# Retention block and FP4 feed-forward: block division on GpSimd, exponents later on VectorE, x rounded in the even body, 11 weight pieces

## What is computed

```python
def fp4_quant_dequant(x):                      # blocks of 16 along the last dim
    xb = x.reshape(shape[:-1] + (shape[-1] // 16, 16))
    scale = jnp.maximum(jnp.max(jnp.abs(xb), -1, keepdims=True) / 6.0, 1e-12)
    xn = xb / scale
    idx = jnp.searchsorted(_MID, jnp.abs(xn))  # nearest of 0 .5 1 1.5 2 3 4 6
    return (_GRID[idx] * jnp.sign(xn) * scale).reshape(shape)

x = layernorm(x + retention(x))                # (2, 2048, 256), 8 heads of 32 / 64
h = silu(q(x) @ q(w_gate).T) * (q(x) @ q(w_up).T)      # q = fp4_quant_dequant
x = layernorm(x + q(h) @ q(w_down).T)          # hidden width 704
```

## Time and profile before

| | |
|---|---|
| median of three runs | 673.51 us |
| the profiled execution | 673.45 us, span 671.5 us |
| busy, share of the span | TensorE matmul 588.0 us (88%), VectorE 580.9 (87%), ScalarE 335.6 (50%), GpSimd 187.3 (28%) |
| attention loop, window 240 to 280 us | TensorE busy 39.79 of 40, VectorE 37.26, ScalarE 26.70, GpSimd 15.29, granted TensorE clock 1.00 |
| feed-forward loop, window 520 to 560 us | TensorE 36.03 of 40, VectorE 38.47, clock 1.00 |

### The profile page before, as it was taken

One profiled execution on the slowest core, in us unless ns is written; L12 is line 12 of the kernel. 1 busy time (PEld: TensorE's weight loads), 2 busy tenths in 40 slices (PEclk: granted clock), 3 DMA queues, 4 the chain that ended last, 5 costly groups with the idle time before them and its releaser, 6 DMA issues.

```text
span 671.5 us, 14647 instructions
## 1 busy us (share of the span) xinstructions
PE 588.0 (88%) x4290; PEld 502.6 (75%) x4290; DVE 580.9 (87%) x1439; ACT 335.6 (50%) x869; POOL 187.3 (28%) x230
## 2 busy tenths in 40 slices
PE   3179999999999999999999677779988999999965
PEld 2158888788787878788787566669877888888755
DVE  6056889999999999999998779989999999999996
ACT  3125656666575666666575643224434334433332
POOL 1011124334533444334530203232222222222110
PEclk9779999999999999999999798979999999999998
DMA  6471101110111001110110000000000000000001
GB/s 155 55 230 41 32 25 49 47 39 8 47 47 47 23 23 47 47 39 8 47 31 18 8 8 2 1 0 19 28 16 16 16 16 16 16 16 16 17 16 48
DMA packets 25853, 23.11 MB, mean 34 GB/s; under 512 B 2024, under 2 KB 22760, under 8 KB 25832
## 3 DMA queue, kind: packets, MB, share of 16 engines
q1 hardware_dynamic: 25016, 21.27, 11.3%
q10 hardware_dynamic: 816, 1.57, 0.7%
HBM read 17.56 MB, written 5.28 MB: 34 GB/s over the span
## 4 chain that ended last, share of the span: by engine, by line
DVE 23%; PE 18%; issue 9%; ACT 1%; POOL 1%; DVEq 1%; ACTq 0%; POOLq 0%
PE wide_banks L1182 9%; PE upd_y L1182 5%; DVE shared L800 2%; DVE stats L926 2%; DVE shared L922 2%; DVE shared L993 1%; PE wide_banks L1340 1%; DVE h_amax L782 1%; DVE shared L989 1%; DVE win_lo L913 1%; DVE shared L795 1%; DVE win_lo L910 1%; DVE h_inv L791 1%; DVE h_scale L787 1%; POOL shared L1160 1%
## 5 line engine op out<-in xcount | busy, mean ns | idle before, releaser
L1160 POOL TENSOR_TENSOR shared<-shared,h_scale 128x704 f32<-128x704 bf16 x32 | 44.4, 1387 | 202.5 <-DVE shared L805 196.9
L1182 PE MATMUL wide_banks<-wgu_hi,xq_hi 128*128 128x512 f32 (+1 forms) x192 | 65.1, 421 | 27.8 <-DVE xq_lo L982 27.8
L1182 PE MATMUL wide_banks<-win_hi,x_hi 128*128 128x512 f32 x192 | 68.5, 438 | 12.9 <-DVE win_lo L885 11.0
L442 ACT ACTIVATE shared<-opened,rstd 128x64 f32<-128x64 f32 x256 | 64.7, 335 | 11.0 <-DVE rstd L715 10.7
L413 ACT ACTIVATE shared<-shared 128x704 bf16<-128x704 f32 x32 | 25.3, 790 | 83.4 <-DVE shared L795 83.4
L1241 PEld LDWEIGHTS mixed<-shared 128*128 128x128 f32 x512 | 62.0, 192 | 2.8
L1182 PE MATMUL wide_banks<-win_hi,x_lo 128*128 128x512 f32 x192 | 60.8, 398 | 0.0
L1182 PE MATMUL wide_banks<-win_lo,x_hi 128*128 128x512 f32 x192 | 60.8, 398 | 0.0
L1241 PE MATMUL mixed<-shared 128*128 128x64 f32 x512 | 60.6, 271 | 0.0
L1182 PEld LDWEIGHTS wide_banks<-wgu_hi,xq_hi 128*128 128x128 f32 x192 | 33.1, 200 | 36.0 <-DVE xq_lo L982 33.0
L1182 PE MATMUL wide_banks<-wgu_hi,xq_lo 128*128 128x512 f32 (+1 forms) x192 | 58.9, 389 | 0.0
(11 more groups left out here) (146 smaller groups left out, 1496.3 us busy)
## 6 DMA issues: line engine op xcount, KB each, us to landing
xf<-in_x_feat SPq DMA_DIRECT2D x32, 128.0 KB, 2.2
tab<-in_tables SPq DMA_DIRECT2D x16, 256.0 KB, 2.7
xt<-in_x_tok SPq DMA_DIRECT2D x32, 128.0 KB, 2.1
out<-shared SPq DMA_DIRECT2D x32, 128.0 KB, 1.7
x<-in_w_in ACTq DMA_DIRECT2D x3, 512.0 KB, 5.3
w<-in_w_gu SPq DMA_DIRECT2D x1, 1408.0 KB, 7.8
pow_dram<-powers SPq DMA_DIRECT2D x1, 1056.0 KB
w<-in_w_down SPq DMA_DIRECT2D x1, 704.0 KB, 9.1
```

Source lines behind the costliest of these rows:

```text
L442: last = act.activation(gated[:, b, cols], opened[:, b, cols], ACT.Copy, scale=rstd[:, b, 1 + k:2 + k])
L1160: pool.tensor_tensor(over_blocks(hq[:, b]), over_blocks(h_steps[:, b]), spread(h_fp4["scale"][:, b]), ALU.mult).then_inc(h_fp4["ready"], 1)
L1182: last = pe.matmul(dst, lhs, rhs, start=k == 0, stop=k == len(parts) - 1)
```

## The change

Nothing of what is computed changes. `x_unit` and `w_unit` go from VectorE to GpSimd, in odd bodies behind `split_x`. On VectorE `w_exponent` comes behind the rotation, `x_exponent` behind `apply_gate`. On ScalarE `round_w_from` comes behind `square_heads`; `round_x_from`, with `round_x1` on GpSimd, goes from the odd body to the even body after it, still between `normalise_heads` and `copy_v`. The loop begins at tile 8, so there are 11 pieces of 384 columns. Behind the loops the steps for the last tiles are moved accordingly.

```diff
-LOOP_FROM, LOOP_TO = 3, TILES // 2 - 1
+LOOP_FROM, LOOP_TO = 4, TILES // 2 - 1
...
 # ScalarE, body
-                if piece is not None and b == 1:
-                    round_w_from(piece)
                 if in_turn(n - LAG):
                     copy_gatedT(n - LAG)
...
                 if valid(n - 2):
                     normalise_heads(n - 2, b)
-                if b == 1 and tiles_of(n - 1):
-                    round_x_from(n - 1)
+                if b == 0 and tiles_of(n - 2):
+                    round_x_from(n - 2)
                 if valid(n + 1):
                     copy_v(n + 1, 1 - b)
...
                 if valid(n):
                     square_heads(n)
+                if piece is not None and b == 1:
+                    round_w_from(piece)
...
 # VectorE, body
-                if w and b == 1:
-                    w_unit(piece)
-                    w_exponent(piece)
                 if valid(n):
                     decay_scores(n)
...
-                if x:
-                    x_unit(n - 1)
-                    x_exponent(n - 1)
                 if valid(n + 1):
                     rotate_products(n + 1, 1 - b)
                     rotate_sum(n + 1, 1 - b)
                 if w and b == 0:
                     w_max(piece)
+                if w and b == 1:
+                    w_exponent(piece)
                 if valid(n):
                     apply_gate(n, b)
...
+                if x:
+                    x_exponent(n - 1)
                 if in_turn(n - LAG):
                     add_resid(n - LAG, 1 - b)
...
 # GpSimd
+            def x_unit(n):
+                need(pool, x_fp4["ready"], n - 4)
+                pool.wait_ge(x_fp4["step"], FP4_STEPS // 2 * (n - 4) + 3)
+                pool.tensor_tensor(over_blocks(x_fp4["unit"][:, 0, 0:width(n)]), over_blocks(columns(x1_flat, n)),
+                                   spread(x_fp4["inv"][:, 0:width(n) // BLOCK]), ALU.mult).then_inc(x_fp4["step"], 1)
+
+            def w_unit(piece):
+                pool.wait_ge(w_fp4["step"], FP4_STEPS * piece + 3)
+                pool.tensor_tensor(over_blocks(w_fp4["unit"][:, 0]), over_blocks(w4[:, bass.ds(piece * PIECE, PIECE)]),
+                                   spread(w_fp4["inv"][:]), ALU.mult).then_inc(w_fp4["step"], 1)
...
 # GpSimd, body, behind decay_k and split_x
                 if piece is not None and b == 1:
+                    w_unit(piece)
+                if b == 1 and tiles_of(n - 1):
+                    x_unit(n - 1)
+                if piece is not None and b == 1:
                     round_w4(piece)
-                if b == 1 and tiles_of(n - 1):
-                    round_x1(n - 1)
+                if b == 0 and tiles_of(n - 2):
+                    round_x1(n - 2)
```

## The result

The changed kernel takes 682.4 us (median of four runs, 680.25 to 683.87), the kernel before on the same chip 673.66 (673.32 to 674.2): ratio 1.0126, 95% interval 1.0095 to 1.0157. It is slower, by 8.7 us where 15.3 were forecast.

A forecast was written before the change was run, and what follows sets the result against it. TensorE's 10.55 us pace and VectorE's hand-overs were taken as the bound. Bodies of 11.15 and 11.85 make pairs +1.41, eleven times +15.5, less 0.2: +15.3 on 673.45, so 688.7 us; range 673 to 692.5.

The forecast's parts named there:

- the forecast case: Whole kernel: the outcome the prediction held likeliest, 685.5 to 692 us, chance 0.52.
- The two hand-overs: VectorE to TensorE: decay_scores to project_v is free up to 3.10 us, decay_q to turn_gated up to 2.12.
- the 0.51 between L617 and L1265 was chance: Doubt that TensorE really waits for decay_q before turn_gated; it decides the rival of freed VectorE time, chance 0.09.
- VectorE's time was the bound and is freed: Rival for the loop: both bodies run at 10.55 us, −5.9 us in all, 667.6 us; chance 0.09.
- The late squares: Even body: x's rounding ahead of square_heads adds 0.54, apply_gate starts 0.98 before the odd body, q becomes 2.88.
- The stall at `split_x` in the odd body: VectorE's L736 waits for GpSimd's split_x: +0.54, q 3.42, odd body 11.85 us.
- x_exponent behind L1134: End of body: x_exponent, issued 0.12 too late, waits for GpSimd's first add; L632 starts at −0.35 instead of −1.09.
- GpSimd's queue in the even body: Add, scale, decay_k and split_x delay VectorE's joint chain: decay_scores at 3.7 instead of 2.99, even body 11.15 us.
- only the stall at `split_x` is missing: Rival: even body 11.15, odd 11.31, so pair +0.87 and 682.9 us, range 680 to 685.5; chance 0.16.
- Tile 7's body: Tiles 6 and 7 have no weights with 11 pieces of 384: about −0.2 us.
- outside the pairs: Edges: tile 31's last rounding of x moves into the start of the feed-forward part; taken as 0, ±1 us.
- the clock is no term: TensorE: its work per pair stays, busy some 21 of 23 us, so no clock cost was counted.

The follow-up runs named there:

- e1: Changed kernel with x's rounding on ScalarE moved ahead of normalise_heads in the even body; 683.73 us, ratio 1.0143.
- e2: Changed kernel with x_exponent ahead of apply_gate instead of behind it; 679.64 us, ratio 1.008.
- e3: Changed kernel with x's rounding ahead of normalise_heads, x_exponent ahead of apply_gate, and decay_q ahead of the two reciprocals; 675.16 us, ratio 1.0012.
- e4: Changed kernel with w_scale and w_inverse moved from the odd body to the even one, right behind w_max; 697.82 us, ratio 1.0349.
- e6: Changed kernel with one GpSimd line added: split_x of tile n+2 waits for decay_scores of tile n; 673.29 us, ratio 0.9983.
- e8: Changed kernel with split_x held until decay_scores and x_exponent ahead of apply_gate; 671.87 us, ratio 0.9969.
- e9: Changed kernel with split_x held until decay_scores, x_exponent ahead of apply_gate and decay_q ahead of the two reciprocals; 668.3 us, ratio 0.9917.
- e7: Changed kernel with x's rounding ahead of normalise_heads, x_exponent ahead of apply_gate, decay_q ahead of the reciprocals, and split_x held until decay_scores; 666.43 us, ratio 0.9881.
- e5: Kernel before with one GpSimd line added: split_x of tile n+2 waits for decay_scores of tile n; 670.61 us, ratio 0.9949.
- b1: Kernel before with 11 weight pieces of 384 columns and x's rounding (ScalarE and GpSimd) moved to the even body; 682.74 us, ratio 1.0126.

## Why the prediction was right, and where its sizes were off

The mechanism came as forecast, its size didn't. The measured 682.4 is inside the range of 673 to 692.5, but that range is wide; it is outside the 685.5 to 692 of the forecast case.

**The two hand-overs held in every kernel.** With q and a the starts of `decay_q` and `decay_scores` in a body:

| body | q or a | q + 8.43 or a + 7.45 | measured |
|---|---|---|---|
| after, odd | q 3.32 | 11.75 | 11.72 |
| e1, odd | q 3.44 | 11.87 | 11.85 |
| e2, even | a 3.16 | 10.61 | 10.59 |
| e3, odd | q 2.95 | 11.38 | 11.39 |
| e4, odd, clock at 1.00 | q 3.99 | 12.42 | 12.38 |
| e6, odd | q 2.71 | 11.14 | 11.11 |
| e8, odd | q 2.65 | 11.08 | 11.05 |
| e9, odd | q 2.22 | 10.65 | 10.67 |
| e7, odd | q 1.81 | free | 10.55 |
| after, even | a 3.40 | 10.85 | 10.84 |
| e5, odd | a 3.38 | 10.83 | 10.83 |
| b1, odd | a 4.48 | 11.93 | 11.94 |

The rival that the 0.51 between L617 and L1265 was chance is out, and with it "VectorE's time was the bound and is freed": after frees 13 us of VectorE and is slower, e5 moves none of VectorE's work and is faster. (That rival's sentence that VectorE has no idle gap in the pair before leaves out 0.20 us ahead of rstd, L715; nothing hangs on it.)

**The late squares: right.** L643 was forecast 0.98 before the odd body and starts 284.50 − 283.51 = 0.99 before it, behind a wait of 0.59. b1 shows the copy's move as the cause.

**The stall at `split_x` in the odd body: right in kind, another victim.** It was to be before's L736 (L737 in after) for 0.54; it is the next instruction, L759, for 0.46. L737 comes at 286.61 − 284.50 = 2.11, not 2.15, in the same hundredth as `split_x`, and takes its usual 0.17. q is 3.32, not 3.42. In e1 L716 came 0.16 behind the add and lost 0.97, in e3 L737 came 0.05 behind `split_x` and lost 0.54. The Trainium skill, SBUF — State Buffer, section Who interferes with whom, says that whoever issues first keeps the shared port pair for its whole instruction; these rows agree with it but for the end, since L690, L759 and L716 go on some 0.14 us before the recorded end of GpSimd's instruction.

**x_exponent behind L1134: right.** 0.12 late was forecast; it was 294.78 − 294.63 = 0.15, and the instruction took 1.14. e2 took it away and gained 0.25 in the even body.

**GpSimd's queue in the even body: the mis-sized term.** L626 was forecast at 3.7 and starts at 3.40. GpSimd was earlier than in my sum (`split_x` at 275.96 − 273.66 = 2.30 instead of 2.45, ending at 3.02 instead of 3.2), and from the release of L690 to L626 VectorE needs 0.52, not the 0.65 that I added. The even body lasts 10.84 instead of 11.15, the odd one 11.72 instead of 11.85: 0.44 a pair, and more in the first. The eleven pairs cost 10.2 and not 15.5, 5.3 us less than forecast. Tile 7's body gave back 0.47 and not 0.2, and 0.8 us lie outside the pairs (0.35 of it ahead of the loop), where 0, ±1 was forecast. Together that is the 4.8 us from the sum (688.7) to the profiled execution (683.87). The median, 682.4, is lower again because this execution was the slowest of the four.

**The rival "only the stall at `split_x` is missing"** gave 682.9, nearly the measured time, and its 680 to 685.5 holds it, for a wrong reason: the stall is there, and what is smaller is the even body. A time that fits doesn't choose a mechanism; the rows do.

## What to carry to other kernels

Before a step is moved on one engine, look at what it releases on the next: here the copy on ScalarE sets GpSimd's add free, and that meets whatever small VectorE instruction stands there. Where VectorE and GpSimd share a hand-scheduled loop, place GpSimd's instructions as carefully as VectorE's: one wait that moves a 0.73 us instruction beside VectorE work that reads PSUM was worth some 9 us in the changed kernel and 3.8 in the one before, while 13 us less work on VectorE brought nothing as long as that instruction stood where it did. Judge such a line in both kernels (e5 and e6), or its gain passes for the cost of the change. And measure a part of a change alone (b1) before crediting or blaming the whole.

## What the runs showed of the hardware that was not expected

**A wait of the same length cost clock in some bodies and none in others.** I had written that the clock is no term. In e4 TensorE waits 1.8 us for `decay_q`. The window of e4 (columns as above) over the 2 us behind such a wait, in the odd body from 195.84:

```profile
200.31:202.30 1.99, 1.99 (x21) 1.42 (x22) 1.41 (x2) 1.04 (x3) 0.84 (x1) 0.56 0.12 34
```

The same of e4 in the odd body from 220.62:

```profile
225.12:226.90 1.78, 1.78 (x25) 1.44 (x25) 1.47 (x2) 1.09 (x3) 0.83 (x1) 1.00 0.13 37
```

TensorE's timeline of e4 at the start of the two:

```profile
200.31 0.90 PE L1276 MATMUL turn<-ident,shared 128*128 128x128 f32 x4 [1.78 <-DVE qdT L618]
...
225.12 0.63 PE L1276 MATMUL turn<-ident,shared 128*128 128x128 f32 x4 [1.80 <-DVE qdT L618]
```

In the first the granted clock fell to about its lower level (1.2 GHz) for some 4 us and the body took 13.92; in the second, behind a wait as long, it stayed at the upper one (2.4 GHz) and the body took 12.38. Ten of the eleven odd bodies have such a wait (the first waits 1.06 and takes 11.65); the clock fell in five of them, 1.54 us each, which is half of what e4 loses against after. What tells the two apart stays open. In after, with waits of 1.12 us, the window above shows 1.00, and so does the same window of e1, with waits of 1.25.

**Less than 0.1 us of start time decides over a stall.** L737 started in the same hundredth as `split_x` in after and took 0.17; in e3 it started 0.05 behind and took 0.72. Beside x's add rstd (L716) took 0.18 when it started 0.09 ahead (e3) and 1.15 when 0.16 behind (e1). Reductions and instructions that read PSUM kept their length beside GpSimd's (in e9 L663 took 0.46 beside `split_x`, in e7 `w_max` 0.55 beside x's second instruction).
